# Causal masks moved from TensorE matmuls into VectorE's maximum, with the masked scores kept in SBUF

## The chip, the cores and the metric

The kernel runs on one core of one Trainium2 chip. The metric is the device time in microseconds (us) of one execution. Three executions of the kernel before took 2177.60, 2175.18 and 2175.93 us, median 2175.93. TensorE does the matmuls, VectorE (DVE in the rows) and ScalarE (ACT) the work on the elements, GpSimd (POOL) the rest of it, and the DMA queues move data.

## The reference, cut to what matters

The program is one layer of a small language model: embedding and layer norm, an attention with three branches, a mixture of experts. Only the attention is touched. For each of 8 sequences of 512 tokens and each of 16 heads (head size 96):

```python
def _attn(q, k, v, mask=None):
    s = jnp.einsum('bhqd,bhkd->bhqk', q, k) / np.float32(np.sqrt(HD))
    if mask is not None:
        s = jnp.where(mask, s, jnp.float32(-1000000000.0))
    return jnp.einsum('bhqk,bhkd->bhqd', jax.nn.softmax(s, -1), v)
...
causal = ii[:, None] >= ii[None, :]
o1 = _attn(q, k1, v1, causal[None, None])        # all earlier tokens
o2 = _attn(q, ks, vs)                            # 128 selected tokens, no mask
winmask = causal & (ii[:, None] - ii[None, :] < WINDOW)
o3 = _attn(q, kw, vw, winmask[None, None])       # a window of 128 tokens
```

## The kernel before, in words

Each engine has its program written out by hand, and semaphores order the engines against each other. The attention is a stream of *units*: a unit is one tile of 128 queries (t = 0 to 3) of one head, so 4 units make a head and 8 x 16 x 4 = 512 units make the attention. For a unit the scores of the three branches stand side by side in one of two PSUM buffers, `S[0]` and `S[1]`, which take turns: n1 = (t+1) x 128 columns of branch 1, 128 of branch 2, n3 = 128 (t = 0) or 256 of branch 3. In blocks of 128 columns that is 3, 5, 6 and 7 blocks for t = 0, 1, 2, 3. The stages of a unit U are:

1. TensorE `scores` (L1070 to L1074): the query tile against the three key sets in fp32 (L1070, L1072, L1073), and two small bf16 matmuls, identity times a table of 0 and -1e30, that add the masks onto the last 128 columns of branch 1 (L1071) and onto the n3 columns of branch 3 (L1074). It waits for `probs_ready`, by which `S` has been read.
2. VectorE `maxima` (L763 to L765): three reduces of `S` to negative row maxima `negm`. It waits for `scores_ready` alone.
3. ScalarE `probs` (L464): three activations exp(S + negm), from `S` in PSUM into the SBUF buffer `pr` (two of them, shown as `big` in rows). It waits for `max_ready`, and for `pT_psum`, by which the unit two back has been read out of the same `pr`.
4. TensorE `turn_probs` (L1082): 3, 5, 6 or 7 transposes of `pr` into the one PSUM buffer `PT`. It waits for `pT_sb`, by which the unit in front has been taken out of `PT`.
5. ScalarE `take_hi` (L475), then VectorE `take_lo` (L773): `PT` is scaled and split in a high and a low fp16 half; two instructions each.
6. TensorE `values` (L1097): the fp16 matmuls with the values, into `O`. At the end of a head VectorE's `combine` (L781 to L786) and GpSimd's `branch_sum` take `O`.

The stages are staggered. In its slot t, working on head H, TensorE issues: one step of work for coming heads (s_turn L1036, q_proj L1006, k_proj L1014/L1016 or q_turn L1023), `scores` of unit u+3, at t = 0 also `k_turn` (L1030, which needs ScalarE's copy of `ksT`, L413), `turn_probs` of unit u+1, `values` of unit u. ScalarE in the same slot: one or two copies out of PSUM (L413), `take_hi` of u+1, `probs` of u+3. VectorE: `maxima` of u+3, then `take_lo` of u+1, and at t = 3 `combine`. Every queue is worked off in that order. A loop handles two heads in one pass; 14 of the 16 heads of a sequence run in it, the last two are written out, with the start of the next sequence between (`behind`).

Of the kernel before, what the change touches and what calls it, by code (L numbers as in the profile page):

```python
# [5 lines left out]
B, T, C = 8, 512, 64  # L6
P = 128
# [17 lines left out]
K_ID, K_MASK, K_COS, K_SIN, K_IOTA, K_TRI, K_END = 0, 128, 384, 704, 1024, 1152, 1216  # L25
# [8 lines left out]
def tower(nc, d, out):  # L34

    fp32, bf16, fp16, i32 = mybir.dt.float32, mybir.dt.bfloat16, mybir.dt.float16, mybir.dt.int32
    ALU, ACT, AX = mybir.AluOpType, mybir.ActivationFunctionType, mybir.AxisListType
    ds = bass.ds
    ctx = ExitStack()
    with ctx:  # L40
        def sb(name, shape, dt=fp32):
            return ctx.enter_context(nc.sbuf_tensor(name, shape, dt))

        def ps(name, shape):
            return ctx.enter_context(nc.psum_tensor(name, shape, fp32))
# [5 lines left out]
        cst = sb("cst", [P, K_END])  # L51
        ident = cst[:, K_ID:K_ID + P]
# [1 line left out]
        sin5 = cst[:, K_SIN:K_SIN + 5 * ROPE].rearrange("p (t r) -> p t r", t=5)  # L54
        iota_row = cst[:, K_IOTA:K_IOTA + P]
        tri = cst[:, K_TRI:K_TRI + NE * NE].rearrange("p (a b) -> p a b", a=NE)
        identb = sb("identb", [P, P], bf16)
        maskb = sb("maskb", [P, 2 * P], bf16)
        ones = sb("ones", [P, P])
        gamma_b = sb("gamma_b", [P, C])  # L60
        beta_b = sb("beta_b", [P, C])
# [73 lines left out]
        pr = [work[:, i * NPR:(i + 1) * NPR] for i in range(2)]  # L135
# [7 lines left out]
        kwT = [sb(f"kwT{i}", [P, T]) for i in range(2)]  # L143
# [5 lines left out]
        negm = [sb(f"negm{i}", [P, 3]) for i in range(2)]  # L149
# [14 lines left out]
        S = [ps(f"S{i}", [P, 1024]) for i in range(2)]  # L164
# [54 lines left out]
        def kblocks(t):  # L219

            return (t + 1) * P, KEEP, (P if t == 0 else 2 * P)
# [189 lines left out]
        def _(act):  # L411
# [6 lines left out]
            k = 0  # L418
            for b_lo, b_hi in PARTS:
                n = (b_hi - b_lo) * NT  # L420
# [8 lines left out]
                for b in range(b_lo, b_hi):  # L429
                    for k2 in range(2):  # L430
                        act.wait_ge(s["lat_psum"], 2 * b + k2 + 1)
                        src = [S[1], PT][b % 2][:, 512 * k2:512 * k2 + 2 * (LAT + 3)].rearrange("p (t c) -> p t c", t=2)
                        n = b * NT + 2 * k2
                        for t in range(2):
# [4 lines left out]
                                                 accum_out=st[:, 5, TILES + n + t:TILES + n + t + 1])  # L439
# [17 lines left out]
            def probs(u, t, b, U):  # L457

                n1, n2, n3 = kblocks(t)
                par = u % 2  # L460
                act.wait_ge(s["max_ready"], U + 1)
                act.wait_ge(s["pT_psum"], U + 1)
                for k, (lo, n) in enumerate(((0, n1), (4 * P, n2), (5 * P, n3))):
                    last = nc.scalar.activation(pr[par][:, lo:lo + n], S[par][:, lo:lo + n], ACT.Exp,  # L464
                                                bias=negm[par][:, k:k + 1])
                last.then_inc(s["probs_ready"], 1)

            def take_hi(u, t, U):
# [102 lines left out]
            for b in range(B):  # L571
                for i, (b_lo, b_hi) in enumerate(PARTS_FFN):
                    if b == (0, 2)[i]:
                        act.wait_ge(s["var_ready"], 2 * len(PARTS) + 2 + i)
                        n = (b_hi - b_lo) * NT
# [31 lines left out]
        def _(dve):  # L607
            v = nc.vector
            ch = Chain(dve, "dve_chain")
            L = ch.link  # L610
            dve.sem_inc(s["comb_done"], 1)
            dve.sem_inc(s["pT_sb"], 1)
            dve.sem_inc(s["ffn_hs"], 4)

# [12 lines left out]


            dve.wait_ge(s["ld_cst"], 16)
            v.tensor_copy(identb[:], ident)  # L630
            L(v.tensor_copy(maskb[:], cst[:, K_MASK:K_MASK + 2 * P]))
            dve.wait_ge(s["ld_w"], 16 * N_W)
            sm = float(HD) ** -0.5
            L(v.tensor_scalar(qw_col[:], qw_col[:], sm, None, ALU.mult))
# [8 lines left out]
            for g_ in range(4):  # L643
                last = v.tensor_copy(wknBD[32 * g_:32 * g_ + 32, :, 32 * g_:32 * g_ + 32],
                                     S[0][32 * g_:32 * g_ + 32, 512:512 + 4 * CKV].rearrange("p (c q) -> p c q", c=4))
# [5 lines left out]
            for buf, rows in ((xnT_all, C), (wlat, C), (wq, CQ), (wv, CKV), (wkw, C), (wks, C), (wvw, C), (wvs, C),  # L651
# [4 lines left out]
                last = v.memset(buf[rows:P], 0.0)  # L656
# [4 lines left out]
            for i, buf in enumerate((wv, wvw, wvs)):  # L661
                last = v.tensor_reduce(vrow[:, i:i + 1], buf[:], op=ALU.max, axis=AX.X, apply_absolute_value=True)
# [8 lines left out]
            def bc(ap, shape):  # L671
                return ap.to_broadcast(shape)
# [26 lines left out]
            for i, (b_lo, b_hi) in enumerate(PARTS):  # L699

                n0, n1 = b_lo * NT, b_hi * NT
# [37 lines left out]
            a, z = sc0, sc1  # L739
            for r in range(KEEP // 8):  # L740
# [3 lines left out]
                a, z = z, a  # L744
# [13 lines left out]
            def maxima(u, t, U):  # L758

                par = u % 2  # L760
                n1, n2, n3 = kblocks(t)
                dve.wait_ge(s["scores_ready"], U + 1)
                v.tensor_reduce(negm[par][:, 0:1], S[par][:, 0:n1], op=ALU.max, axis=AX.X, negate=True)  # L763
                v.tensor_reduce(negm[par][:, 1:2], S[par][:, 4 * P:4 * P + n2], op=ALU.max, axis=AX.X, negate=True)  # L764
                v.tensor_reduce(negm[par][:, 2:3], S[par][:, 5 * P:5 * P + n3], op=ALU.max, axis=AX.X, negate=True).then_inc(s["max_ready"], 1)  # L765

            def take_lo(u, t, U):

# [98 lines left out]
            n = TILES * NE  # L867
# [4 lines left out]
            m = st[:, 4, 0:TILES]  # L872
# [10 lines left out]
            for a_ in range(NE):  # L883
                mine = bc(e3[:, :, a_:a_ + 1], [P, TILES, NE])
                v.tensor_tensor(big4[:, :, a_, :], e3, mine, ALU.is_gt)
                last = v.tensor_tensor(eq4[:, :, a_, :], e3, mine, ALU.is_equal)
            L(last)
            for a_ in range(NE):
                last = v.tensor_tensor(eq4[:, :, a_, :], eq4[:, :, a_, :], bc(tri[:, a_:a_ + 1, :], [P, TILES, NE]), ALU.mult)
# [10 lines left out]
            for i in range(2):  # L900
                L(v.tensor_copy(cpart_b, c3))
                L(v.tensor_copy(cparts[:, :, i, :], cpart_b))
                last = v.tensor_tensor(c3 if i == 0 else cparts[:, :, 2, :], c3, cparts[:, :, i, :], ALU.subtract)
# [32 lines left out]
        def _(pe):  # L936
            mm, tp = nc.tensor.matmul, nc.tensor.transpose
# [5 lines left out]
            for a, src in enumerate((xf, instr, argsf)):  # L943
                for t in range(NT):
                    o = (a * NT + t) * B
                    last = tp(X[:, o:o + B], src[:, t * P:(t + 1) * P], cst[0:B, 0:B])
# [6 lines left out]
            for c in range(4):  # L953
                last = tp(S[0][:, 512 + c * CKV:512 + (c + 1) * CKV], wkn[:, c * P:(c + 1) * P], cst[0:CKV, 0:CKV])
            last.then_inc(s["wT_psum"], 1)
            pe.wait_ge(s["wT_sb"], 1)
            for c in range(4):
                last = mm(S[1][0:CQ, c * P:(c + 1) * P], wqnT[:, c, :], wknBD[:, c, :], start=True, stop=True)
# [21 lines left out]
            for i, (b_lo, b_hi) in enumerate(PARTS):  # L980
                pe.wait_ge(s["xn_ready"], i + 1)
                transposes("xnT_psum", "xnT_sb", b_lo, b_hi)
                for b in range(b_lo, b_hi):
                    pe.wait_ge(s["xnT_sb"], b + 1)
                    mm(O[0:B, :], wimp[:, B - 1 - b:2 * B - 1 - b], xnT_all[:, b * T:(b + 1) * T], start=(b == 0),
                       stop=(b == B - 1)).then_inc(s["imp_psum"], 1)
                for b in range(b_lo, b_hi):
                    if b >= 2:
                        pe.wait_ge(s["lat_sb"], 2 * (b - 1))
                    for t in range(NT):  # L990
                        n_ = (b * NT + t) * P
                        o = (t // 2) * 512 + (t % 2) * (LAT + 3)
                        last = mm([S[1], PT][b % 2][:, o:o + LAT + 3], xnT_all[:, n_:n_ + P], wlat[:], start=True, stop=True)
# [69 lines left out]

            def scores(u, t, par, U):

                pe.wait_ge(s["probs_ready"], U + 1)
                z = S[u % 2]
                n1, n2, n3 = kblocks(t)
                q = qT[par][:, t * P:(t + 1) * P]
                mm(z[:, 0:n1], q, k1T[:, 0:n1], start=True, stop=True)  # L1070
                mm(z[:, n1 - P:n1], identb[:], maskb[:, P:2 * P], start=False, stop=True, skip_group_check=True)  # L1071
                mm(z[:, 4 * P:5 * P], q, ksT[par][:], start=True, stop=True)  # L1072
                mm(z[:, 5 * P:5 * P + n3], q, kwT[par][:, (t + 1) * P - n3:(t + 1) * P], start=True, stop=True)  # L1073
                mm(z[:, 5 * P:5 * P + n3], identb[:], maskb[:, 2 * P - n3:2 * P], start=False, stop=True, skip_group_check=True).then_inc(s["scores_ready"], 1)  # L1074

            def turn_probs(u, t, U):
                pe.wait_ge(s["probs_ready"], U + 3)
# [125 lines left out]
            for t in range(NT):  # L1203
                last = tp(S[0][:, t * B:(t + 1) * B], rankm[:, t * P:(t + 1) * P], cst[0:B, 0:B])
# [20 lines left out]
            for c in range(4):  # L1225
                if c >= 2:
                    pe.wait_ge(s[["oT_act", "oT_dve"][c % 2]], (B - 1) * 2 + 1)
                for t in range(NT):
                    last = tp(PT[:, (c % 2) * 512 + t * P:(c % 2) * 512 + (t + 1) * P], o_b[:, t, c * P:(c + 1) * P], ident)
# [61 lines left out]
            for b in range(B):  # L1291
                if b >= 2:
                    pe.wait_ge(s["cT_sb"], b - 1)
                for t in range(NT):
                    last = tp(PT[0:3 * NE, (b % 2) * 512 + t * P:(b % 2) * 512 + (t + 1) * P],
                              cparts[:, b * NT + t].rearrange("p a e -> p (a e)"), ident)
# [63 lines left out]
```

## Time and profile before

| | before |
|---|---|
| median of three runs | 2175.93 us |
| the profiled execution, its own time | 2175.96 us |
| its span on the core | 2174.2 us |
| TensorE busy, matmul / weight load | 1933.2 us (89%) / 1579.1 us (73%) |
| VectorE busy | 1296.0 us (60%) |
| ScalarE busy | 1332.8 us (61%) |
| GpSimd busy | 1019.8 us (47%) |
| chain that ended last, by engine | PE 85%, issue 6%, DVE 5%, ACT 2% |

The attention fills the span from about 245 to 2020 us. There TensorE is busy in nine tenths or more of every slice of the page, and VectorE and ScalarE in some six and seven tenths. The shares are of one profiled execution. A matmul's end in the rows is modelled and holds its run through the array, so the start of the next row, not its end, tells how long TensorE's queue was held.

### The profile page before, as it was taken

To read this page: it belongs to the slowest core of one execution; us is meant where nothing else is said; L and a number is where in the kernel's file an instruction comes from. 1 tells how busy PE (TensorE), PEld (TensorE's weight loads), DVE (VectorE), ACT (ScalarE), POOL (GpSimd) and SP (SyncE) were. 2 spreads that over 40 slices of the span, in tenths; PEclk is the share of its full clock that TensorE was granted. 3 is DMA by queue.
4 is the path that set the end of the run, shared out by engine and by line. 5 is a ranking of instruction groups with operands and counts; after the bars stand their busy time and mean duration, and the time that the engine had idled before them with its cause. 6 is when DMAs were issued, how large, how long until landed. Compare 5 with 4: busy or idle time off the path is not lost.

```text
span 2174.2 us, 56981 instructions
## 1 busy us (share of the span) xinstructions
PE 1933.2 (89%) x19452; PEld 1579.1 (73%) x19452; DVE 1296.0 (60%) x3336; ACT 1332.8 (61%) x3520; POOL 1019.8 (47%) x1680
## 2 busy tenths in 40 slices
PE   1123899999999999999999999999999999999769
PEld 0011688878887888788878888888888887888522
DVE  4417466656665666566666666666656665666443
ACT  0022477767776777677766776677767776777232
POOL 6743355535553555445544555455445544554000
PEclk9956799999999999999999999999999999999579
DMA  4100000000000000000000000000000000000000
GB/s 80 25 12 14 12 0 0 2 12 0 0 0 13 0 0 0 13 0 0 0 13 0 0 0 13 0 0 0 13 0 0 0 2 1 0 0 0 1 5 14
DMA packets 21980, 13.51 MB, mean 6 GB/s; under 512 B 17401, under 2 KB 18425, under 8 KB 21953
## 3 DMA queue, kind: packets, MB, share of 16 engines
q1 hardware_dynamic: 18880, 10.03, 1.8%
q0 software_dynamic: 3072, 3.15, 0.8%
q8 instruction: 14, 0.23, 0.0%
q14 instruction: 14, 0.11, 0.0%
HBM read 6.34 MB, written 1.05 MB: 3 GB/s over the span
## 4 chain that ended last, share of the span: by engine, by line
PE 85%; issue 6%; DVE 5%; another core or an unknown queue 2%; ACT 2%; ACTq 0%; DMA 0%; POOLq 0%; DVEq 0%; POOL 0%
PE PT L1082 13%; PE S L1070 13%; PE O L1097 9%; PE S L1073 9%; PE X L1006 7%; PE S L1072 6%; PE X L1014 5%; PE S L1145 3%; PE X L1030 3%; PE X L1023 3%; PE S L1074 2%; PE O L1273 1%; PE O L1192 1%; PE S L1253 1%
## 5 line engine op out<-in xcount | busy, mean ns | idle before, releaser
L464 ACT ACTIVATE big<-S,negm 128x128 f32<-128x128 f32 (+3 forms) x1536 | 576.1, 455 | 49.8 <-DVE negm L765 49.7
L475 ACT ACTIVATE big<-PT 128x384 f16<-128x384 f32 (+3 forms) x1024 | 405.4, 448 | 313.7 <-PE PT L1082 311.9
L773 DVE SCALAR_TENSOR_TENSOR big<-PT,big 128x384 f16<-128x384 f32 (+3 forms) x1024 | 477.1, 503 | 177.7 <-ACT big L475 177.6
L763 DVE TENSOR_REDUCE negm<-S 128x1 f32<-128x128 f32 (+3 forms) x512 | 251.6, 491 | 378.8 <-PE S L1074 377.7
L1082 PE MATMUL PT<-cst,big 128*128 128x128 f32 x2688 | 379.7, 274 | 6.6 <-DVE big L773 6.6
L1070 PE MATMUL S<-k1T,qT 128*128 128x128 f32 (+3 forms) x1024 | 368.8, 442 | 0.6 <-ACT big L464 0.3
L1082 PEld LDWEIGHTS PT<-cst,big 128*128 128x128 f32 x2688 | 303.9, 141 | 41.9 <-issue 5.9
L363 POOL TENSOR_TENSOR osum<-big 128x128 f32<-128x128 f32 x128 | 61.7, 482 | 535.9 <-DVE big L786 535.9
L1097 PEld LDWEIGHTS O<-vh,big 128*128 128x128 f16 x8064 | 277.6, 96 | 15.1 <-issue 8.0
L1097 PE MATMUL O<-vh,big 128*128 128x33 f16 x8064 | 282.3, 178 | 1.4 <-DVE big L773 1.4
L1073 PE MATMUL S<-kwT,qT 128*128 128x256 f32 (+1 forms) x1024 | 278.9, 354 | 0.0
L1072 PE MATMUL S<-ksT,qT 128*128 128x128 f32 x1024 | 225.3, 302 | 0.0
L1072 PEld LDWEIGHTS S<-ksT,qT 128*128 128x128 f32 x1024 | 154.6, 191 | 87.8 <-issue 71.2
L344 POOL TENSOR_TENSOR big<-qs,cst 128x256 f32<-128x256 f32 x128 | 93.1, 727 | 248.6 <-ACT qs L413 248.6
L765 DVE TENSOR_REDUCE negm<-S 128x1 f32<-128x256 f32 (+1 forms) x512 | 195.4, 382 | 0.0
L1070 PEld LDWEIGHTS S<-k1T,qT 128*128 128x128 f32 x1024 | 156.8, 193 | 1.6 <-ACT big L464 0.7
L1073 PEld LDWEIGHTS S<-kwT,qT 128*128 128x128 f32 x1024 | 155.5, 192 | 0.0
L1006 PE MATMUL X<-wq,cqT 128*128 (+1 forms) x1024 | 149.2, 289 | 4.4 <-ACT qs L413 0.7
L1014 PE MATMUL X<-wkw,xnT_b 128*128 (+1 forms) x1024 | 143.9, 284 | 1.1 <-issue 1.1
L413 ACT ACTIVATE kwT<-X 128x512 f32<-128x512 f32 x128 | 76.4, 597 | 110.9 <-PE X L1030 110.9
L764 DVE TENSOR_REDUCE negm<-S 128x1 f32<-128x128 f32 x512 | 143.7, 281 | 0.0
L1006 PEld LDWEIGHTS X<-wq,cqT 128*128 128x128 f32 x1024 | 125.5, 193 | 16.1 <-ACT k1n L413 1.1
(252 smaller groups left out, 3012.5 us busy)
## 6 DMA issues: line engine op xcount, KB each, us to landing
lat_b<-lat_all SPq DMA_DIRECT2D x8, 448.0 KB, 2.8
xn_b<-xn_all SPq DMA_DIRECT2D x8, 128.0 KB, 2.5
xnT_b<-xnT_all SPq DMA_DIRECT2D x8, 128.0 KB, 2.3
out_dram<-h_all SPq DMA_DIRECT2D x8, 128.0 KB, 2.0
cst<-in_c_cst_dram SPq DMA_DIRECT2D x1, 608.0 KB, 5.1
big<-in_L_tok_token_emb_dram,idx POOLq DMA_INDIRECT x32
big<-in_L_tok_instr_emb_dram,idx POOLq DMA_INDIRECT x32
big<-in_L_tok_arg_emb_dram,idx POOLq DMA_INDIRECT x32
```

What stands on the lines that cost most here:

```text
L464: last = nc.scalar.activation(pr[par][:, lo:lo + n], S[par][:, lo:lo + n], ACT.Exp, bias=negm[par][:, k:k + 1])
L475: nc.scalar.activation(pT[par][:, 0, lo:lo + n], PT[:, lo:lo + n], ACT.Copy, scale=PSCALE).then_inc(s["pT_hi"], 1)
L763: v.tensor_reduce(negm[par][:, 0:1], S[par][:, 0:n1], op=ALU.max, axis=AX.X, negate=True)
L765: v.tensor_reduce(negm[par][:, 2:3], S[par][:, 5 * P:5 * P + n3], op=ALU.max, axis=AX.X, negate=True).then_inc(s["max_ready"], 1)
L773: last = v.scalar_tensor_tensor(pT[par][:, 1, lo:lo + n], PT[:, lo:lo + n], PSCALE, pT[par][:, 0, lo:lo + n], ALU.mult, ALU.subtract)
L1006: last = mm(X[:, t * QW:(t + 1) * QW], cqT[:, t * P:(t + 1) * P], wq[:].rearrange("c h q -> c (h q)")[:, ds(h * QW, QW)], start=True, stop ...
L1014: mm(X[:, t * HD:(t + 1) * HD], xnT_b[:, t * P:(t + 1) * P], wkw[:].rearrange("c h q -> c (h q)")[:, ds(h * HD, HD)], start=True, stop=True)
L1070: mm(z[:, 0:n1], q, k1T[:, 0:n1], start=True, stop=True)
L1072: mm(z[:, 4 * P:5 * P], q, ksT[par][:], start=True, stop=True)
L1073: mm(z[:, 5 * P:5 * P + n3], q, kwT[par][:, (t + 1) * P - n3:(t + 1) * P], start=True, stop=True)
L1082: last = tp(PT[:, lo:lo + P], src[:, lo:lo + P], ident)
L1097: last = mm(o, w[:, c, blocks[i] * P:(blocks[i] + 1) * P], vh[p][:, a, v0 + i, :], start=(j == 0), stop=(j == len(parts) - 1))
```

## The change

The two mask matmuls of `scores` are gone, with their bf16 tables `identb` and `maskb`. In their place VectorE has fp32 tables in SBUF: `mask_w`, a part of the constants that were loaded anyway, and `mask_c`, 384 zeros followed by the causal table. `maxima` is no longer three reduces but three `tensor_tensor_reduce`: each reads a part of `S` and the mask beside it, writes -(S + mask) to `pr` in SBUF, and gives the smallest of these values, which is the negative maximum, as `negm`. As it now writes `pr`, `maxima` of unit U waits for `pT_psum` (the transposes of unit U-2 out of the same buffer), and a nop stands behind the two waits. `probs` reads `pr` in place of `S`, with scale -1, in place, and no longer waits for `pT_psum`. `scores` waits for `max_ready` of unit U-2 in place of its `probs_ready`.

```diff
-        identb = sb("identb", [P, P], bf16)
-        maskb = sb("maskb", [P, 2 * P], bf16)
+        mask_w = cst[:, K_MASK:K_MASK + 2 * P]
+        mask_c = sb("mask_c", [P, T])
...
-                act.wait_ge(s["max_ready"], U + 1)
-                act.wait_ge(s["pT_psum"], U + 1)
+                act.wait_ge(s["max_ready"], U + 3)
                 for k, (lo, n) in enumerate(((0, n1), (4 * P, n2), (5 * P, n3))):
-                    last = nc.scalar.activation(pr[par][:, lo:lo + n], S[par][:, lo:lo + n], ACT.Exp,
-                                                bias=negm[par][:, k:k + 1])
+                    last = nc.scalar.activation(pr[par][:, lo:lo + n], pr[par][:, lo:lo + n], ACT.Exp,
+                                                bias=negm[par][:, k:k + 1], scale=-1.0)
...
+            dve.sem_inc(s["max_ready"], 2)
...
-            v.tensor_copy(identb[:], ident)
-            L(v.tensor_copy(maskb[:], cst[:, K_MASK:K_MASK + 2 * P]))
+            v.memset(mask_c[:, 0:T - P], 0.0)
+            L(v.tensor_copy(mask_c[:, T - P:T], cst[:, K_MASK + P:K_MASK + 2 * P]))
...
-                v.tensor_reduce(negm[par][:, 0:1], S[par][:, 0:n1], op=ALU.max, axis=AX.X, negate=True)
-                v.tensor_reduce(negm[par][:, 1:2], S[par][:, 4 * P:4 * P + n2], op=ALU.max, axis=AX.X, negate=True)
-                v.tensor_reduce(negm[par][:, 2:3], S[par][:, 5 * P:5 * P + n3], op=ALU.max, axis=AX.X, negate=True).then_inc(s["max_ready"], 1)
+                dve.wait_ge(s["pT_psum"], U + 1)
+                dve.nop(nofuse=True)
+                for k, (lo, n, m) in enumerate(((0, n1, mask_c[:, T - n1:T]), (4 * P, n2, mask_c[:, 0:n2]),
+                                                (5 * P, n3, mask_w[:, 2 * P - n3:2 * P]))):
+                    z = S[par][:, lo:lo + n]
+                    last = v.tensor_tensor_reduce(out=pr[par][:, lo:lo + n], in0=z, in1=m, scale=-1.0, scalar=3.0e38, op0=ALU.add, op1=ALU.min,
+                                                  accum_out=negm[par][:, k:k + 1])
+                last.then_inc(s["max_ready"], 1)
...
-                pe.wait_ge(s["probs_ready"], U + 1)
+                pe.wait_ge(s["max_ready"], U + 1)
...
                 mm(z[:, 0:n1], q, k1T[:, 0:n1], start=True, stop=True)
-                mm(z[:, n1 - P:n1], identb[:], maskb[:, P:2 * P], start=False, stop=True, skip_group_check=True)
                 mm(z[:, 4 * P:5 * P], q, ksT[par][:], start=True, stop=True)
-                mm(z[:, 5 * P:5 * P + n3], q, kwT[par][:, (t + 1) * P - n3:(t + 1) * P], start=True, stop=True)
-                mm(z[:, 5 * P:5 * P + n3], identb[:], maskb[:, 2 * P - n3:2 * P], start=False, stop=True, skip_group_check=True).then_inc(s["scores_ready"], 1)
+                mm(z[:, 5 * P:5 * P + n3], q, kwT[par][:, (t + 1) * P - n3:(t + 1) * P], start=True, stop=True).then_inc(s["scores_ready"], 1)
```

## Rows read from the trace of the kernel before

**Rows 1.** Windows view, attention: busy us (instructions) of each engine, granted clock.

```profile
core 0: us, PE busy (x) PEld busy (x) DVE busy (x) ACT busy (x) POOL busy (x), PEclk, DMA share, GB/s
469.00:680.00 211.00, 208.71 (x2284) 179.54 (x2283) 135.42 (x367) 151.40 (x399) 103.71 (x178) 1.00 0.01 3
```

**Rows 2.** Page, costliest groups: busy us, mean ns | idle before, releaser.

```profile
L1070 PE MATMUL S<-k1T,qT 128*128 128x128 f32 (+3 forms) x1024 | 368.8, 442 | 0.6 <-ACT big L464 0.3
```

**Rows 3.** Timeline, TensorE: start us, length us, line; three-block transposes, two heads apart.

```profile
987.75 0.49 PE L1082 MATMUL PT<-cst,big 128*128 128x128 f32 x3
...
1013.66 0.49 PE L1082 MATMUL PT<-cst,big 128*128 128x128 f32 x3
```

**Rows 4.** Timeline, TensorE: transposes, k_proj's slot with its mask matmuls, transposes.

```profile
1006.89 0.82 PE L1082 MATMUL PT<-cst,big 128*128 128x128 f32 x6
...
1009.57 0.22 PE L1071 MATMUL S<-maskb,identb 128*128 128x128 bf16 x1
...
1009.62 0.44 PE L1072 MATMUL S<-ksT,qT 128*128 128x128 f32 x2
...
1010.33 0.27 PE L1074 MATMUL S<-maskb,identb 128*128 128x256 bf16 x1
...
1010.44 0.93 PE L1082 MATMUL PT<-cst,big 128*128 128x128 f32 x7
```

**Rows 5.** Timeline, VectorE and ScalarE beside the end of rows 4.

```profile
1010.64 0.42 DVE L763 TENSOR_REDUCE negm<-S 128x1 f32<-128x256 f32 x1 [1.26 <-PE S L1074]
...
1011.18 0.41 DVE L765 TENSOR_REDUCE negm<-S 128x1 f32<-128x256 f32 x1
...
1011.41 0.98 ACT L475 ACTIVATE big<-PT 128x512 f16<-128x512 f32 x2 [1.47 <-PE PT L1082]
...
1012.03 1.16 DVE L773 SCALAR_TENSOR_TENSOR big<-PT,big 128x512 f16<-128x512 f32 x2 [0.44 <-ACT big L475]
```

**Rows 6.** Timeline, slots t = 3 and t = 0, from maxima to take_lo.

```profile
1013.86 0.56 DVE L763 TENSOR_REDUCE negm<-S 128x1 f32<-128x384 f32 x1 [0.67 <-PE S L1074]
...
1014.98 1.20 ACT L464 ACTIVATE big<-S,negm 128x384 f32<-128x384 f32 x3 [0.24 <-DVE negm L765]
...
1016.07 0.28 ACT L413 ACTIVATE ksT<-X 128x128 f32<-128x128 f32 x1
...
1016.40 0.42 PEld L1030 LDWEIGHTS X<-cst,kk 128*128 128x128 f32 x4 [0.23 <-ACT ksT L413]
...
1016.60 0.69 DVE L763 TENSOR_REDUCE negm<-S 128x1 f32<-128x512 f32 x1
...
1016.89 0.71 PE L1082 MATMUL PT<-cst,big 128*128 128x128 f32 x5
...
1017.40 0.41 DVE L765 TENSOR_REDUCE negm<-S 128x1 f32<-128x256 f32 x1
...
1018.05 0.94 DVE L773 SCALAR_TENSOR_TENSOR big<-PT,big 128x256 f16<-128x256 f32 x2 [0.24 <-ACT big L475]
```

**Rows 7.** Groups by shape, VectorE: a reduce, and an operation with two inputs.

```profile
L764 DVE TENSOR_REDUCE negm<-S 128x1 f32<-128x128 f32 x512 | 143.7, 281 | 0.0
L773 DVE SCALAR_TENSOR_TENSOR big<-PT,big 128x128 f16<-128x128 f32 x128 | 36.0, 281 | 0.0
```

**Rows 8.** Timeline before the attention: ScalarE's accumulator read, and VectorE's short companion instruction.

```profile
142.27 0.19 ACT L437 ACTIVATION_READ_ACCUMULATOR vall<-S 128x1 f32 x1
142.37 0.19 ACT L438 ACTIVATE vall<-S 128x32 f32<-128x32 f32 x1
...
192.36 0.08 DVE L743 MATCH_VALUE_LOAD o_b<-oT,o_b 8x8 f32 x1
```

**Rows 9.** Waits view, GpSimd: us in total, times, longest us.

```profile
POOL o_b L365 <- POOL osum L363: 19.7, 112, 0.2
...
POOL vh L372 <- POOL vh L369: 17.0, 112, 0.2
```

**Rows 10.** Groups by shape, ScalarE: small operations from PSUM and from SBUF.

```profile
L413 ACT ACTIVATE gl_all<-S 128x6 f32<-128x6 f32 x8 | 2.0, 251 | 0.0
L424 ACT ACTIVATE st<-st 128x8 f32<-128x8 f32 x4 | 1.4, 343 | 16.9 <-DVE st L694 16.9
```

## The prediction, made before the changed kernel was run

> **What bounds the kernel now.** I read the page's slices first, to find the attention, then one window of it. There TensorE has 208.71 us of matmul in 211.00 us, at a granted clock of 1.00 (the 2.4 GHz level), VectorE 135.42 and ScalarE 151.40 [rows 1]. So TensorE's queue sets the pace, and what is cut from it is time won, as long as nothing else comes late. Next I asked whether the wait that the change loosens costs anything: the first score matmul stood idle for 0.6 us in all 1024 rows [rows 2], so an earlier release of the score bank is worth nothing. What is left are two things: the mask matmuls, and the new place of `maxima` on VectorE. For them I read the timeline of two heads. A head takes (1013.66 - 987.75) / 2 = 12.96 us [rows 3].
>
> **What goes from TensorE.** A mask matmul holds the queue from its own start to the next one's: L1071 from 1009.57 to 1009.62, 0.05 us, L1074 (256 columns) from 1010.33 to 1010.44, 0.11 us [rows 4]. The row's length (0.22, 0.27) is the run through the array and would say four times as much. With 128 columns, at t = 0, I take 0.05 for L1074 too. A head saves 3 x 0.16 + 0.10 = 0.58 us, and 128 heads 74 us, 3.4% of the time. This is all that the edit can give, and only while TensorE's queue stays the bound: 2175.96 - 74 = 2102 us.
>
> **What the new wait does.** Today `maxima` of u+3 starts when its scores are in, while TensorE is still at the transposes of u+1 behind them: L763 starts at 1010.64, the seven transposes run to 1010.44 + 0.93 = 1011.37 [rows 4, 5]. It is over (1011.18 + 0.41 = 1011.59) before `take_lo` can start at all, which waits for ScalarE's `take_hi` (from 1011.41) [rows 5]. So the maxima are nearly free. After the change they wait for those same transposes (`pT_psum`), because they write into the buffer that the transposes read. Queued behind them on VectorE is `take_lo` of u+1, and for that wait TensorE's next `turn_probs` (one `PT`) and `values`. ScalarE's `probs` come behind the maxima too, and behind these its copy of `ksT`, for which `k_turn` waits already today (0.23 us idle) [rows 6]. The maxima thus move from beside the path onto it: transposes, maxima, take_lo, next transposes. I close the ring over one head, with today's lengths:
>
> 1. Slot t = 3: three transposes 0.49 [rows 3], and 0.04 until another engine starts, as from 1011.37 to 1011.41 [rows 4, 5]: 0.53.
> 2. The maxima of a 6-block unit, from L763 to the start of `probs`, 1014.98 - 1013.86 = 1.12 [rows 6].
> 3. ScalarE's `probs`, then the copy of `ksT`, to 1016.07 + 0.28 = 1016.35: 1.37; TensorE starts at 1016.40: 1.42 together [rows 6].
> 4. `k_turn` and five transposes, from 1016.40 to 1016.89 + 0.71 = 1017.60, and 0.04: 1.24 [rows 6].
> 5. Maxima of a 7-block unit, 1016.60 to 1017.40 + 0.41 = 1.21, then `take_lo` 0.94, less 0.08 of overlap, and 0.05 until TensorE starts: 2.12 [rows 6]. The overlap is that of the reduces: 0.42 + 0.28 + 0.41 = 1.11 in lengths are 0.95 from first start to last end, over two joins [rows 5, 7]. The `take_hi` on ScalarE is covered by the maxima.
> 6. TensorE alone sets the slots t = 1 and 2: from the six transposes to the end of the seven, 1011.37 - 1006.89 = 4.48, less both masks 0.16, and 0.04: 4.36 [rows 4]. In it VectorE's work of slot 1 is hidden. (In slot 3 the `take_lo` and `combine` that follow the maxima lie beside steps 3 and 4, 2.66 us in which the ring doesn't need VectorE.)
> 7. Maxima of a 5-block unit 0.95, `take_lo` 1.16, less 0.08, and 0.05: 2.08 [rows 5].
>
> The sum is 0.53 + 1.12 + 1.42 + 1.24 + 2.12 + 4.36 + 2.08 = 12.87 us, against 12.96 now. Of the 0.58 us cut from TensorE only 0.09 are left, even if the new VectorE instructions cost no more than the reduces. The turn of the two-head loop, which is in the 12.96, is covered here, since TensorE waits for ScalarE at that place.
>
> **What the new instruction costs.** The trace has no `tensor_tensor_reduce`. Its stream of elements I take as that of a reduce: an operation with one input from PSUM, one from SBUF and an output to SBUF takes 281 ns for 128 columns, just as the reduce does [rows 7]. On top comes the accumulated minimum. On ScalarE an accumulated result is an instruction of its own; the next one starts 0.10 us behind its start (142.27 to 142.37), and it is 0.19 us long [rows 8]. A short companion instruction on VectorE takes 0.08 us [rows 8]. Bounds: 0, if the result comes out with the operation, and 0.19, if nothing of such an instruction overlaps. I take 0.09, between the two nearest rows. It stands nine times in the ring (steps 2, 5 and 7, three each): 0.81 us a head, and 1.71 at the upper end.
>
> The Trainium skill, "VectorE: DVE Perf Modes", section "Two Vector instructions with no wait between them", speaks for the same side: a VectorE operation that also writes out its accumulator is two instructions, the main one and an accumulator read. It gives no time, and no run here shows it yet.
>
> The nop behind the waits: on GpSimd the pair of copies with a nop in between waits 17.0 us in 112 times, the pair without one 19.7 [rows 9], so nothing; at most 0.05 us in each of three places of the ring. `probs` from SBUF in place of PSUM: 343 ns against 251 ns in the nearest small operations [rows 10], which are of different functions; between 0 and 0.09 us a head (once, at the end of step 3); I take 0. The memset and the copy at the start take the place of two copies ahead of the weights' arrival: nothing.
>
> **The sum.** A head: 12.87 + 0.81 - 12.96 = +0.72 us. It holds for the heads in the loop and the first of the two written out, 15 x 8 = 120: +86 us. The other 32 units (the last head of a sequence and the start of the next) keep gaining their masks, 0.16 each: -5 us. VectorE has there room between the units, so I add nothing. 2175.96 + 86 - 5 = 2257 us. The median of the runs, 2175.93, is the same to 0.03 us.
>
> **The rivals.**
> - *The accumulated result is free* (0 in place of 0.09): 120 x -0.09 = -11, and -5: 2160 us, faster. Against it speaks ScalarE's row, for it that the operation is another engine's. The point where the sign turns is low: 16 us of gain over 120 x 9 instructions is 0.015 us each.
> - *TensorE stays the bound*: the ring has slack that I don't see (the transposes could fall earlier beside other work), and the masks' time is won whole: 2102 us. For it speaks that VectorE is busy for only 64% of the attention [rows 1]; against it that the order of the queue, not the load, makes the ring.
> - *The instruction is dear*: 0.15 to 0.19 us each, nothing overlapping. 9 x 0.15 - 0.09 = 1.26 a head, 151 - 5: 2322 us; with 0.19, 120 x 1.62 - 5: 2365 us.
> - *Half rate*: the operation streams one element in two cycles. 18 blocks stand in the ring (steps 2, 5, 7: 6, 7 and 5); a block more costs (0.69 - 0.42) / 2 = 0.135 us, by the reduces of 512 and 256 columns [rows 5, 6], so 2.4 us a head, 292 us on top: 2549 us. The Trainium skill, "Vector Engine (DVE) Microarchitecture Reference", section "Points that are easy to get wrong", states such a halving for two SBUF sources that are not bf16. Here one source is PSUM, so by that rule it doesn't apply.
> - *The change does less than it says*: that the score bank comes free sooner is true and worth 0.6 us [rows 2]; it is in every case above.
>
> **How the numbers follow.** Forecast case, accumulator read of 0.05 to 0.12 us, 2214 to 2290 us: 0.55. Dear: 0.15. Free or nearly, 2145 to 2171: 0.15. Between the two, within 0.2% of now (about what a measurement of this kernel can tell from no change): 0.07. TensorE the bound: 0.05. Half rate: 0.03. Slower 0.55 + 0.15 + 0.03 = 0.73, same 0.07, faster 0.20. The range from 2145 to 2335 leaves out half rate, the full gain and the dearer half of the dear case, some 0.16; the likeliest case's own is 2214 to 2290.
>
> **What would show each step.** Masks: TensorE's matmul rows fall by 1024, and its busy share of an attention window from 99% to some 93%. New wait: idle time before L1082 with VectorE's `take_lo` as its releaser, where there were nearly none, and more before L1030 with `ksT`; the row of `maxima` waits for PE PT L1082, no longer for the scores. The instruction: its length for 128 columns beside 281 ns, and a row of its own for the accumulator between two of them. Slot 1: no wait before the seven transposes. The granted clock stays 1.00; if the new gaps make it fall, all numbers are too low. The prediction is wrong at its root if TensorE doesn't wait for `take_lo`, and in size if the accumulator costs other than 0.09 us.

## The result, and the profile after

The changed kernel takes 2272.46 us (median of four runs, 2271.38 to 2274.52) beside 2175.55 us for the kernel before: ratio 1.0447, 95% interval 1.0430 to 1.0463, slower by 97 us. The forecast was 2257 us, slower, in a range of 2145 to 2335. The sign and the mechanism came out. The size came out too, but in part by luck: of the two large terms behind it one was too high and one too low, and the experiments were needed to see that.

The windows view of the kernel after, in the same stretch as rows 1 (busy us of each engine, granted clock):

```profile
core 0: us, PE busy (x) PEld busy (x) DVE busy (x) ACT busy (x) POOL busy (x), PEclk, DMA share, GB/s
469.00:680.00 211.00, 197.53 (x2027) 162.90 (x2024) 123.23 (x515) 150.18 (x369) 103.87 (x179) 1.00 0.00 1
```

TensorE's share fell from 99% [rows 1] to 94%, and no engine took its place: VectorE is at 58%. The clock stayed at its upper level. So engines wait for each other. The waits view of the kernel after names them (engine, line, releaser: us in total, times, longest us):

```profile
PE X L1035 <- ACT ksT L413: 58.1, 119, 1.2
PE PT L1085 <- DVE big L778: 37.9, 137, 1.8
...
PEld X L1035 <- ACT ksT L413: 106.3, 120, 1.6
PEld PT L1085 <- issue: 61.4, 124, 1.9
...
PEld PT L1085 <- DVE big L778: 56.0, 126, 1.2
```

L1035 is `k_turn` and L1085 `turn_probs` (L1030 and L1082 before), L778 is `take_lo`. The waits for `ksT` and for `take_lo` are those at the ends of the prediction's steps 3 and 5, and they stand in nearly every head (119 to 137 times). So does the wait that the view puts down to "issue": it stands before the three transposes, at the end of step 7 (see the last two rows of the timeline below). On VectorE's side, the costliest groups of the page show that the maxima now wait for the transposes:

```profile
L768 DVE CUSTOM_DVE_ANT_0 big<-S,mask_c 128x128 f32<-128x128 f32 (+3 forms) x1024 | 359.9, 389 | 640.7 <-PE PT L1085 620.0
L1075 PE MATMUL S<-k1T,qT 128*128 128x128 f32 (+3 forms) x1024 | 369.1, 442 | 0.2 <-ACT vall L413 0.2
```

The second row answers to rows 2: the earlier release of the score bank brought the wait from 0.6 to 0.2 us, which is nothing, as forecast.

A head, from one set of three-block transposes to the set two heads on, is (1038.28 - 1010.97) / 2 = 13.66 us, against 12.96 [rows 3]:

```profile
1010.97 0.52 PE L1085 MATMUL PT<-cst,big 128*128 128x128 f32 x3
...
1038.28 0.52 PE L1085 MATMUL PT<-cst,big 128*128 128x128 f32 x3
```

And this is the ring itself in the timeline of the kernel after, slots t = 3 and t = 0, to be laid beside rows 6:

```profile
1011.53 0.55 ACT L474 ACTIVATE big<-PT 128x128 f16<-128x128 f32 x2
1011.62 0.56 DVE L768 CUSTOM_DVE_ANT_0 big<-S,mask_c 128x384 f32<-128x384 f32 x1 [0.80 <-PE PT L1085]
...
1012.78 1.31 ACT L463 ACTIVATE big<-big,negm 128x384 f32<-128x384 f32 x3 [0.70 <-DVE negm L768]
...
1013.99 0.25 ACT L413 ACTIVATE ksT<-X 128x128 f32<-128x128 f32 x1
1014.30 0.42 PEld L1035 LDWEIGHTS X<-cst,kk 128*128 128x128 f32 x4 [0.63 <-ACT ksT L413]
...
1014.79 0.71 PE L1085 MATMUL PT<-cst,big 128*128 128x128 f32 x5
...
1015.63 0.69 DVE L768 CUSTOM_DVE_ANT_0 big<-S,mask_c 128x512 f32<-128x512 f32 x1 [1.33 <-PE PT L1085]
...
1016.25 0.08 DVE L768 DVE_READ_ACCUMULATOR2_ANT negm<- 128x1 f32 x1
1016.25 0.29 DVE L768 CUSTOM_DVE_ANT_0 big<-S,mask_c 128x128 f32<-128x128 f32 x1
...
1016.81 0.08 DVE L768 DVE_READ_ACCUMULATOR2_ANT negm<- 128x1 f32 x1
1016.81 0.88 DVE L778 SCALAR_TENSOR_TENSOR big<-PT,big 128x256 f16<-128x256 f32 x2
...
1017.74 0.64 PEld L1085 LDWEIGHTS PT<-cst,big 128*128 128x128 f32 x6 [0.36 <-DVE big L778]
1017.75 0.87 PE L1085 MATMUL PT<-cst,big 128*128 128x128 f32 x6 [0.17 <-DVE big L778]
...
1019.06 1.13 PE L1019 MATMUL X<-wkw,xnT_b 128*128 x8
...
1023.33 1.15 DVE L778 SCALAR_TENSOR_TENSOR big<-PT,big 128x512 f16<-128x512 f32 x2
...
1024.60 0.31 PEld L1085 LDWEIGHTS PT<-cst,big 128*128 128x128 f32 x3 [0.48 <-issue]
```

Each stage starts where the one in front ends, and `ksT`'s copy (to 1014.24) and `take_lo` (to 1017.69) each release TensorE after an idle time. At the end of step 7 `take_lo` ends at 1023.33 + 1.15 = 1024.48 and the three transposes' weight load follows 0.12 us later. That distance is the median of the kernel after and also of e2, e5, e8 and e9 below, in some of which the view names ScalarE's `probs`, for which these transposes don't wait by the code. So the ring closes through `take_lo`, as predicted. The accumulator read is an instruction of its own, 0.08 us long, but it starts together with the next operation (both rows say 1016.25, and again 1016.81), so it takes next to no room in the queue.

### The profile page after: what moved, and what is told of

It reads as the page before. It is cut to its first block and busy times, and to the rows that moved or that the text cites. A ratio compares the mean times of both kernels' runs of the same rounds, so it can differ in the third digit from the quotient of the medians.

```text
span 2269.5 us, 56582 instructions
## 1 busy us (share of the span) xinstructions
PE 1915.0 (84%) x18428; PEld 1523.7 (67%) x18428; DVE 1278.3 (56%) x4872; ACT 1409.3 (62%) x3520; POOL 1018.2 (45%) x1680
## 5 line engine op out<-in xcount | busy, mean ns | idle before, releaser
L463 ACT ACTIVATE big<-big,negm 128x128 f32<-128x128 f32 (+3 forms) x1536 | 627.9, 471 | 196.5 <-DVE negm L768 179.6
L768 DVE CUSTOM_DVE_ANT_0 big<-S,mask_c 128x128 f32<-128x128 f32 (+3 forms) x1024 | 359.9, 389 | 640.7 <-PE PT L1085 620.0
L778 DVE SCALAR_TENSOR_TENSOR big<-PT,big 128x384 f16<-128x384 f32 (+3 forms) x1024 | 469.4, 500 | 27.0 <-ACT big L474 26.9
L1085 PE MATMUL PT<-cst,big 128*128 128x128 f32 x2688 | 388.6, 277 | 50.0 <-DVE big L778 37.9
L1085 PEld LDWEIGHTS PT<-cst,big 128*128 128x128 f32 x2688 | 302.1, 141 | 133.8 <-issue 61.4
L1076 PEld LDWEIGHTS S<-ksT,qT 128*128 128x128 f32 x1024 | 184.8, 190 | 101.7 <-issue 61.2
L768 DVE CUSTOM_DVE_ANT_0 big<-S,cst 128x256 f32<-128x256 f32 (+1 forms) x512 | 197.8, 386 | 0.0
L1076 PE MATMUL S<-ksT,qT 128*128 128x128 f32 x1024 | 197.0, 274 | 0.0
L1019 PEld LDWEIGHTS X<-wkw,xnT_b 128*128 128x128 f32 x1024 | 125.5, 193 | 21.2 <-issue 21.2
```

What stands on the lines that cost most here:

```text
L463: last = nc.scalar.activation(pr[par][:, lo:lo + n], pr[par][:, lo:lo + n], ACT.Exp, bias=negm[par][:, k:k + 1], scale=-1.0)
L768: last = v.tensor_tensor_reduce(out=pr[par][:, lo:lo + n], in0=z, in1=m, scale=-1.0, scalar=3.0e38, op0=ALU.add, op1=ALU.min, accum_out=ne ...
L778: last = v.scalar_tensor_tensor(pT[par][:, 1, lo:lo + n], PT[:, lo:lo + n], PSCALE, pT[par][:, 0, lo:lo + n], ALU.mult, ALU.subtract)
L1019: mm(X[:, t * HD:(t + 1) * HD], xnT_b[:, t * P:(t + 1) * P], wkw[:].rearrange("c h q -> c (h q)")[:, ds(h * HD, HD)], start=True, stop=True)
L1085: last = tp(PT[:, lo:lo + P], src[:, lo:lo + P], ident)
```

## The experiments

The ring theory: the changed kernel loses because the maxima must wait for the transposes. The rivals: the new VectorE operation is what costs; or TensorE's masks were never worth anything. The kernel before was timed again beside each group of experiments: 2174.48 us with e1, e2, e3 and e5, 2175.27 with e6, e8, e9 and e10, 2174.95 with e11, e12 and e13.

**One part alone, each on its own.** e1 is the kernel before without the two mask matmuls, e2 the kernel before with only the new wait, e5 has both, and e3 is the changed kernel with the wait taken out of effect by more buffers.

```diff
 # e1_masks_gone, and e5_wait_no_masks
-                mm(z[:, n1 - P:n1], identb[:], maskb[:, P:2 * P], start=False, stop=True, skip_group_check=True)
-                mm(z[:, 5 * P:5 * P + n3], identb[:], maskb[:, 2 * P - n3:2 * P], start=False, stop=True, skip_group_check=True)
 # e2_wait_only, and e5_wait_no_masks: in maxima
                 dve.wait_ge(s["scores_ready"], U + 1)
+                dve.wait_ge(s["pT_psum"], U + 1)
```

> The kernel before with both mask matmuls left out and nothing in their place: the scores go unmasked, so this leaves out the causal and window masks. Ring theory (the change loses through the place of the maxima, not through TensorE's work): TensorE's queue stays the bound, and 0.58 us a head are won, 128 times: 2102 us, 2098 to 2115 if the wait for the copy of ksT comes late in some heads. Rival (TensorE's masks were hidden all along): 2170 or more.

2090.95 us, ratio 0.9611 (0.9595 to 0.9627): 83.5 us are won, more than the 74 of the forecast (the two masks together are worth 0.16 us to a unit, where I had 0.15 in the mean). Part of the surplus lies at the turn of the two-head loop: in the traces a head with that turn takes 0.32 us longer than one without it in the kernel before (13.10 against 12.78), and 0.13 longer in e1 (12.29 against 12.16). The masks were real work on TensorE's queue.

> The kernel before, complete, masks on TensorE, reduces on VectorE; the one edit is that the maxima wait for the transposes of the unit two back (pT_psum), as after the change. Ring theory: the ring of the prediction, 12.87, plus the masks that stand in its TensorE stretch, 0.16, plus up to 0.24 a head for k_proj, which in the changed kernel waits for a copy of ScalarE behind the late probs: 13.03 to 13.27 a head against 12.96, so 2184 to 2213 us. Instruction theory (the new VectorE operation is what costs): 2176, no change.

2255.52 us, ratio 1.0362 (1.0344 to 1.0379). The wait alone makes the kernel 81 us slower, with not one new instruction in it. The instruction theory is refuted as the main cause. But it is 42 us above the top of what my ring gave, so the ring was too short.

> The two edits above together: masks left out (causal and window masks are missing), reduces kept, maxima wait for the transposes. It is the changed kernel with the old VectorE operation, without its nop, and with probs from PSUM. Ring theory: 12.87 to 13.11 a head: 2160 to 2190 us, so some 80 of the 97 us between the full gain of the masks and the changed kernel's time must show here, at 60 to 90 us over e1. Instruction theory: the same as e1, 2102.

2223.04 us, ratio 1.0220 (1.0203 to 1.0237): 132 us above e1. The wait eats the masks' whole gain and 49 us more. Again it is longer than expected (2190 at most).

```diff
 # e3_four_buffers, on the changed kernel
-        pr = [work[:, i * NPR:(i + 1) * NPR] for i in range(2)]
+        pr = [work[:, i * NPR:(i + 1) * NPR] for i in range(2)] + [sb(f"pr{i}", [P, NPR])[:] for i in range(2)]
-        negm = [sb(f"negm{i}", [P, 3]) for i in range(2)]
+        negm = [sb(f"negm{i}", [P, 3]) for i in range(4)]
-            pe.sem_inc(s["pT_psum"], 2)
+            pe.sem_inc(s["pT_psum"], 4)
 # take_hi waits for U + 5; pr[par] and negm[par] become pr[u % 4] and negm[u % 4] in maxima, probs and turn_probs
```

> The changed kernel, complete, with four buffers for pr and negm in place of two, so that the maxima wait for the transposes of the unit four back, which are long done. Nothing else changes: same VectorE operation, same nop, same probs from SBUF. Ring theory: TensorE's queue is the bound again, 2102 to 2135 us, faster than both kernels. Instruction theory: 2272 as the changed kernel, since all its instructions are the same.

2122.11 us, ratio 0.9748 (0.9732 to 0.9765). With the same instructions, nop and all, the changed kernel is 150 us faster once its maxima needn't wait, and beats the kernel before by 52 us. In its waits view VectorE waits for the scores again, no longer for the transposes:

```profile
DVE big L768 <- PE S L1077: 239.3, 247, 2.0
...
DVE pr L768 <- PE S L1077: 93.7, 186, 1.0
...
PEld X L1035 <- ACT ksT L413: 70.9, 120, 1.3
```

**Where the ring was mis-measured.** The two-head distance in e5 gives a head of (1033.31 - 1006.74) / 2 = 13.29 us, where my ring without an accumulator has 12.87. Its timeline shows why. The first fence is the stretch that I had given to TensorE alone (step 6):

```profile
1000.01 0.87 PE L1081 MATMUL PT<-cst,big 128*128 128x128 f32 x6
1000.39 0.60 ACT L413 ACTIVATE qs<-X 128x512 f32<-128x512 f32 x1
...
1001.00 0.29 DVE L764 TENSOR_REDUCE negm<-S 128x1 f32<-128x128 f32 x1 [1.04 <-PE PT L1081]
...
1001.24 1.13 PE L1015 MATMUL X<-wkw,xnT_b 128*128 x8
```

From the six transposes to `k_proj` (L1015) it is 1001.24 - 1000.01 = 1.23 us, in the kernel after 19.06 - 17.75 = 1.31; before the change it was 1.04 (from 1006.89 [rows 4] to this row of the kernel before, which stood among no rows of the prediction):

```profile
1007.93 1.11 PE L1014 MATMUL X<-wkw,xnT_b 128*128 x8
```

`k_proj` waits for ScalarE's copy `qs` (to 1000.99), which stands in ScalarE's queue behind the `probs` of the same slot, and these behind the late maxima. That is a second path through the same maxima. The other part is lag: the maxima start 0.07 us behind ScalarE's `take_hi`, though the same transposes release both:

```profile
1004.50 0.98 ACT L475 ACTIVATE big<-PT 128x512 f16<-128x512 f32 x2 [1.31 <-PE PT L1081]
1004.57 0.42 DVE L764 TENSOR_REDUCE negm<-S 128x1 f32<-128x256 f32 x1 [1.96 <-PE PT L1081]
```

I had put 0.04 us for each hand-over, from ScalarE's `take_hi` [rows 4, 5]. With its one old wait VectorE too started 0.04 us behind the scores (1010.33 + 0.27 = 1010.60, then 1010.64 [rows 4, 5]); with the second wait it is 0.10 behind the transposes. `take_hi` has two waits as well, so their number alone doesn't explain this, and the cause stays open.

**The terms of the new instruction.** Between e5 (2223) and the changed kernel (2272) lie the nop, the read of `probs` from SBUF and the VectorE operation.

```diff
 # e8_nop_added: e5, and in maxima
                 dve.wait_ge(s["pT_psum"], U + 1)
+                dve.nop(nofuse=True)
 # e9_probs_from_psum: the changed kernel, mask table all zeros
-                    last = nc.scalar.activation(pr[par][:, lo:lo + n], pr[par][:, lo:lo + n], ACT.Exp, bias=negm[par][:, k:k + 1], scale=-1.0)
+                    last = nc.scalar.activation(pr[par][:, lo:lo + n], S[par][:, lo:lo + n], ACT.Exp, bias=negm[par][:, k:k + 1])
-                pe.wait_ge(s["max_ready"], U + 1)
+                pe.wait_ge(s["probs_ready"], U + 1)
```

> e5_wait_no_masks with the changed kernel's nop behind the two waits of the maxima, and nothing else; so it too leaves out the causal and window masks. It prices the nop. In the changed kernel's trace the maxima start 0.09 to 0.13 us behind the transposes that release them, in e5 0.07 to 0.11. Theory A (the nop costs that difference): 0.02 to 0.03 us at three or four places of the ring, 0.1 us a head, 2223 + 12 = 2235 us. Theory B (the nop is free, as the prediction took it): 2223.

2221.08 us (2219.7 to 2222.85), e5 had 2223.04 (2221.89 to 2223.23). The nop is free, as the prediction had it; the 0.02 to 0.03 us a place that I expected here as theory A were not borne out.

> The changed kernel with probs reading the scores from PSUM again (scale 1, and so scores wait for probs_ready again), and a mask table of zeros, so that no mask is applied (causal and window masks are left out). VectorE's operation, nop and wait stay. It prices the read from SBUF: three activations take 1.31 and 1.41 us in the changed kernel where they took 1.20 and 1.31 in the kernel before. Theory A (the 0.10 us stand twice in the ring, ahead of the copy of ksT and ahead of the copy of qs, for which k_proj waits): 2272 - 120 x 0.2 = 2248 us. Theory B (only ahead of ksT, as the prediction's ring has it): 2260. Theory C (the loss is in VectorE's operation): 2272.

2248.64 us, 24 below the changed kernel: theory A to the microsecond. Three activations are 0.10 us longer in the changed kernel (1.31 us for 6 blocks in the ring above, 1.20 in rows 6), and this counts twice a head, ahead of `ksT` and ahead of `qs`. The edit changes more than the source, though: the activations also lose their scale of -1 and no longer work in place, and no run separates these from the read of SBUF. The later release of the score bank, which comes back with the edit, is worth nothing by the waits above. What is left between e8 and e9, 27.6 us or 0.23 a head, is the VectorE operation. Its rows in the kernel after by shape:

```profile
L768 DVE DVE_READ_ACCUMULATOR2_ANT negm<- 128x1 f32 x1536 | 127.8, 83 | 0.0
L768 DVE CUSTOM_DVE_ANT_0 big<-S,mask_c 128x512 f32<-128x512 f32 x128 | 88.6, 692 | 163.6 <-PE PT L1085 158.4 <-issue 5.1
```

The operation on 512 columns takes 692 ns, the reduce took 0.69 us [rows 6]: it is as fast as the reduce. A set of maxima takes 1.16 us to the start of `probs` (1011.62 to 1012.78) where it took 1.12 [rows 6]: 0.04 us more a set, and three of the four sets of a head stand in the ring (steps 2, 5 and 7), 0.12 us. The rest is the start of the set. In e8, with the same waits and the same nop, the reduce starts 0.09 us behind the end of the transposes (1017.35 + 0.52 = 1017.87, then 1017.96):

```profile
1017.35 0.52 PE L1082 MATMUL PT<-cst,big 128*128 128x128 f32 x3
...
1017.96 0.56 DVE L765 TENSOR_REDUCE negm<-S 128x1 f32<-128x384 f32 x1 [0.76 <-PE PT L1082]
```

The new operation starts 0.13 us behind it (1010.97 + 0.52 = 1011.49, then 1011.62 in the kernel after; e9's median is the same). Three such hand-overs stand in the ring (steps 1, 4 and 6), another 0.12 us. Together that is the 0.23, to the rounding; why the operation starts later than the reduce stays open.

**Is TensorE's queue still part of it?** The masks put back on TensorE, beside VectorE's:

```diff
 # e6_masks_back, on the changed kernel
+                mm(z[:, n1 - P:n1], identb[:], maskb[:, P:2 * P], start=False, stop=True, skip_group_check=True)
+                mm(z[:, 5 * P:5 * P + n3], identb[:], maskb[:, 2 * P - n3:2 * P], start=False, stop=True, skip_group_check=True)
```

> The changed kernel, complete, with the two bf16 mask matmuls put back on TensorE beside VectorE's masks (masked columns are then lowered twice, which changes nothing in the result). Ring theory: of the four scores of a head only those in the ring's TensorE stretch count, so the masks cost about as much as between e5 and e2, 32 us, and not the 84 us that they are worth where TensorE is the bound (kernel before against e1): 2296 to 2305 us. If TensorE's queue is the bound of the changed kernel: 2356.

2301.53 us, 29 above the changed kernel. The same two matmuls cost 83.5 us where TensorE is the bound (e1), 32.5 between e5 and e2, and 29 here: only what stands in the ring's TensorE stretch counts.

**The ring through ScalarE.** If it is real, it must give way when ScalarE's copies go ahead of `probs`, with the wait left as it is.

```diff
 # e12_ksT_early_two_buffers: ScalarE, turn(); the same copy at t = 0 goes, and one stands in behind() ahead of probs(2, 2)
+                    if last == 0 and t == 3:
+                        evac(ksT[p][:], X[:, 0:KEEP], xb + 5 + x_index(0, "sT"))
                     if last < 2 or t < 1:
                         probs(u + 3, (t + 3) % NT, b, U + t + 3)
 # e11_qs_early_two_buffers: likewise, the same copy at t = 1 goes
+                    if last == 0 and t == 0:
+                        evac_q(p, xb + x_index(0, "qp"))
```

> The changed kernel, complete, two buffers, with the one edit that ScalarE copies ksT of the next head ahead of the probs of slot t = 3. It cuts ScalarE out of the ring's steps 2 and 3. From the start of the three transposes to the start of k_turn the changed kernel takes about 3.3 us; TensorE's own queue there takes 2.74 and 3.15 us in the kernel before, less 0.16 for the masks, so 2.79 in the mean. Ring theory: 0.54 us a head, 120 times, 65 us: 2207 us. If the ring goes through VectorE there as well (maxima, take_lo of three blocks), it is only some 20 to 40 us: 2235 to 2250. Without a ring through ScalarE: 2272.

2187.05 us, 85 below the changed kernel, and some 20 more than expected. It is still 12 us above the kernel before (ratio 1.0052, interval 1.0035 to 1.0068): with two buffers the change doesn't pay. The surplus is in the stretch from the three transposes to `k_turn`: over the heads in the loop it takes 2.50 us in the mean, where I expected 2.79 and the changed kernel has 3.37; 0.16 of this is lost again before the six transposes. The wait for `ksT` is gone from the waits, the one for `take_lo` stays (weight loads of e12, L780 is `take_lo`):

```profile
PEld PT L1087 <- DVE big L780: 53.3, 119, 1.3
```

So steps 2 and 3 of the ring were ScalarE's. The place of one 0.28 us copy decides 85 us.

> The changed kernel, complete, two buffers, with the one edit that ScalarE copies qs ahead of the probs of slot t = 0. In the changed kernel's trace k_proj starts 1.31 us behind the six transposes where it was 1.04 before, and 0.24 us behind the end of that copy. If this is a second path of the ring's TensorE stretch, 0.2 us a head go: 2248 us. If the copy is not what k_proj waits for: 2272.

2244.71 us, 28 below the changed kernel (24 expected). The second path is shown.

**The best version.**

> e3_four_buffers, complete, and in addition ScalarE copies ksT of the next head ahead of the probs of slot t = 3 in place of behind them. In e3's trace TensorE's weight load still idles 70.9 us for that copy. If this is the last thing beside TensorE's own queue: 2122 - 30 to 60 = 2062 to 2092 us, and no wait for ksT in the trace; if the waits are the turn of the loop seen under another name, no change, 2122.

e10 is e3 and e12 together. 2074.79 us, ratio 0.9536 (0.9521 to 0.9552): 100.5 us faster than the kernel before. It is also 16 us below e1, which has no masks at all but still waits 37.2 us for `ksT`. TensorE is back at 99% of the window:

```profile
469.00:680.00 211.00, 208.02 (x2252) 181.29 (x2251) 141.86 (x573) 165.79 (x413) 112.53 (x192) 1.00 0.01 3
```

> e10_ksT_early (four buffers, complete) and the copy of qs ahead of the probs of slot t = 0. In e10's trace TensorE is busy in 207.06 of 210 us and no wait for an engine is left that stands in every head, so no more than 5 us are there: 2070 to 2075 us.

2074.08 us (2072.84 to 2075.72): no difference to e10, as expected. With TensorE's queue the bound, `qs` was hidden.

## Why the prediction was right, step by step

**What bounds the kernel.** Right. TensorE's queue; e1 shows it with 83.5 us. The forecast of 74 was 10 low.

**The new wait, the ring.** Right in its stations, save one that it left out, and too short. I had 12.87 us for seven steps. In e5 they are, in order, as medians of its heads and counted from weight load to weight load, 0.66, 1.12, 1.42, 1.31, 2.07, 4.56 and 2.13: 13.27. The steps through VectorE and ScalarE (2 and 3) were exact, step 5 was 0.05 too long. Short were the hand-overs to and from VectorE (steps 1, 4 and 7: by 0.13, 0.07 and 0.05), and step 6 by 0.20. There the sentence "TensorE alone sets the slots t = 1 and 2" failed: `k_proj` waits for `qs`, which I had not followed through ScalarE's queue, though I had done so for `ksT`. From the maxima of the 7-block unit to `k_proj` the longer way is that through ScalarE's `probs` and `qs`; by `take_lo` and the six transposes alone `k_proj` would start some 0.2 us sooner, and with `qs` early it does (e11). Moving the maxima moves all that stands behind `probs`, too.

**The new instruction.** Too dear in one term, forgotten in another. The accumulator read, 0.09 us nine times, 0.81 a head, was the largest addition to the ring in the sum. The read exists and is 0.08 us long, but overlaps the next operation; the whole VectorE operation is worth 27.6 us (e8 against e9), 0.23 a head. The rule of two instructions (the Trainium skill, "VectorE: DVE Perf Modes", section "Two Vector instructions with no wait between them") is borne out by 1536 rows of an accumulator read. That two instructions also take the time of two was my step, and it failed. The half rate was rightly held unlikely: 692 ns for 512 columns, with one source in PSUM and one in SBUF. The read of `probs` from SBUF I took at 0, with 0.09 a head as the upper end; with its scale of -1, and in place, it is 0.20 a head (24 us, e9). The pair of rows that I had for it [rows 10] had nearly the size of three activations, 0.09 against 0.10, but I counted it once. The nop at 0 was right.

**The sum.** By the pair of heads that I had read, a head takes 0.70 us more (13.66 against 12.96), where I had 0.72. Summed over the whole traces, from the weight loads of the three-block transposes of one head to those of the next, the times in us are:

| | before | e1 | e5 | e8 | e9 | after |
|---|---|---|---|---|---|---|
| 112 heads of the loop | 1446.8 | 1369.0 | 1488.5 | 1483.9 | 1509.5 | 1530.9 |
| one of them | 12.92 | 12.22 | 13.29 | 13.25 | 13.48 | 13.67 |
| 8 heads, the first written out | 95.9 | 92.3 | 101.0 | 100.6 | 102.6 | 103.4 |
| from the last head to the next sequence, 7 times | 209.1 | 204.8 | 209.1 | 209.7 | 210.9 | 211.5 |
| the rest of the span | 422.4 | 423.3 | 421.5 | 424.2 | 422.6 | 423.7 |

A head of the loop is 0.75 longer. The parts, in the order e5, e8, e9, after: ring +0.37 where I had -0.09, nop -0.04 where I had 0, operation +0.23 where I had +0.81, `probs` +0.19 where I had 0. So the ring was 0.46 too low, and the instruction with `probs` 0.39 too high. The two all but cancelled, and 2257 was nearer than its working deserved.

**The written-out heads.** For 120 heads I had +86 us; the loop and the first of the two written out lost 84.1 + 7.5 = 91.6. For all that is left I had -5, and this sign was wrong: 2.4 us were lost between the sequences, and 1.3 in the rest. "VectorE has there room between the units" failed as well: between the sequences e1 gains 4.3 us without the masks, and e5, with the wait, gains nothing.

**The rivals.** "The accumulated result is free" was near the truth as to the instruction, and would have made the kernel faster by my ring, which fails: with the ring as measured even e5, with no new operation at all, is 2.2% slower. "The instruction is dear" and "half rate" are refuted by the 0.23 us a head of the whole operation. "TensorE stays the bound" describes e1 and, once the wait is gone, e10. "The change does less than it says" was right in its limit: the release of the score bank is worth nothing.

## What to carry to other kernels

A step that is moved from an engine's queue to another is priced by the dependence that it brings along, not by the busy time of the engine that takes it: here VectorE was busy for under 60% of the attention, and its new wait cost 81 us by itself. Before such a change, write down the ring of engines that each wait for the one in front, and for each station ask what else stands behind it in its queue, down to small copies; more buffers at the place where the ring closes, and copies put ahead of long work, took the same change from 4.5% slower to 4.6% faster. And an operation that is two instructions may hold its queue hardly longer than one: two rows with the same start tell it.

## What the runs showed that I had not expected

- The accumulator read on VectorE starts together with the following operation; 1536 of them, 127.8 us busy, hold the queue for nearly nothing (a set of three is 0.04 us longer than three reduces). On ScalarE such a read held it for 0.10 us [rows 8].
- An Exp on ScalarE that reads SBUF in place with a scale of -1 is slower than one that reads PSUM: 6 blocks in three instructions 1.31 against 1.20 us, 7 blocks 1.41 (kernel after) against 1.31 (kernel before). By e9 it is worth 24 us here; which of the three differences it is, no run shows.
- The maxima, which had started 0.04 us behind what released them, started 0.10 us behind it once they had a second wait (e5), and 0.07 behind a ScalarE instruction that the same event released; a nop between the waits and the operation added nothing (2221 against 2223 us). The new operation started another 0.04 us later than the reduce.
